# Latent attention and FFN on one core: when the main value products run among the score tiles

## The reference

```python
x = x + _layernorm(_L0_attn_ref(_layernorm(x), ...))
x = x + _layernorm(_L0_ffn_ref(_layernorm(x), ...))

# _L0_attn_ref, 16 heads of 128 + 64 (rope) query and key columns, 128 value columns:
scores = jnp.einsum('bhqd,bhkd->bhqk', qf, kf) * scale
probs = jax.nn.softmax(scores)
ctx = jnp.einsum('bhqk,bhkd->bhqd', probs, v)
main_out = ctx.transpose(0, 2, 1, 3).reshape(b, s, H * D_V) @ o_w.T
# beside it a second attention of 16 heads of 16 columns ("pattern"):
p_probs = jax.nn.softmax(jnp.einsum('bhqd,bhkd->bhqk', pq, pk) * PD ** (-0.5))
p_ctx = jnp.einsum('bhqk,bhkd->bhqd', p_probs, pv)
return gates[..., 0:1] * main_out + gates[..., 1:2] * pattern_out
```

## Time and profile before

| what | value |
|---|---|
| median of 3 runs | 790.09 us (786.98 to 792.28) |
| the profiled execution | 788.47 us, its span 786.7 us |
| PE busy | 751.6 us, 96% |
| DVE busy | 574.2 us, 73% |
| ACT busy | 391.9 us, 50% |
| POOL busy | 431.9 us, 55% |

### The profile page before, as it was taken

The page is one execution under the profiler, slowest core; times in us unless marked ns, Lnnn a source line. Parts: engine busy times, 40 slices in busy tenths (PEclk is TensorE's granted clock), DMA queues, the critical chain, the costliest instruction groups (busy, mean ns, idle before and its releaser), DMA issues. The chain is left out here.

```text
span 786.7 us, 13921 instructions
## 1 busy us (share of the span) xinstructions
PE 751.6 (96%) x5508; PEld 473.5 (60%) x5508; DVE 574.2 (73%) x674; ACT 391.9 (50%) x498; POOL 431.9 (55%) x281
## 2 busy tenths in 40 slices
PE   5998899999999999999999999999999999998995
PEld 5875565555555556655655565556655655457884
DVE  6886656775778577847774779577857789998647
ACT  4633455555555455555555555555555445641351
POOL 1253087437843794379437943794378445563343
PEclk9999999999999999999999999999999999998998
DMA  9897740044104430353045103530353312531001
GB/s 242 269 318 239 135 102 14 2 114 91 41 2 84 93 82 1 78 112 96 2 106 110 43 1 77 101 82 1 77 94 93 117 43 53 158 101 35 1 1 54
DMA packets 98169, 68.15 MB, mean 87 GB/s; under 512 B 66806, under 2 KB 76600, under 8 KB 97848
## 3 DMA queue, kind: packets, MB, share of 16 engines
q1 hardware_dynamic: 98104, 67.25, 34.2%
HBM read 41.23 MB, written 17.04 MB: 74 GB/s over the span
## 5 line engine op out<-in xcount | busy, mean ns | idle before, releaser
L1029 POOL TENSOR_TENSOR acc<-acc,em 128x1024 f32<-128x1024 f32 x96 | 234.8, 2446 | 55.0 <-ACT em L1086 52.6
L1170 DVE TENSOR_REDUCE m2p<-xb 128x2 f32<-128x1024 f32 x128 | 155.6, 1221 | 65.1 <-PE xb L1335 65.1
L1178 DVE TENSOR_REDUCE m<-xb 128x2 f32<-128x1024 f32 x128 | 155.8, 1221 | 61.9 <-PE xb L1335 61.5
L1077 ACT ACTIVATE ep<-xb 128x1024 f32<-128x1024 f32 x128 | 131.3, 1026 | 118.6 <-PE xb L1335 118.5
L1086 ACT ACTIVATE em<-xb 128x1024 f32<-128x1024 f32 x128 | 131.3, 1025 | 93.2 <-PE xb L1335 88.8
L1371 PE MATMUL pvm<-em,cpair 128*32 128x512 f32 x1024 | 136.0, 603 | 0.0
L992 POOL TENSOR_TENSOR rot<-rot,sin 128x512 f32<-128x512 f32 x32 | 41.1, 1285 | 121.1 <-DMA rot<-raw 121.1
L1335 PEld LDWEIGHTS xb<-pq,pk 49*128 49x128 f32 x256 | 23.8, 183 | 106.4 <-issue 88.8
L1029 POOL TENSOR_TENSOR acc<-em 128x1024 f32<-128x1024 f32 x16 | 38.2, 2390 | 84.1 <-PE xb L1484 75.9
L1382 PE MATMUL pvp<-ep,vp 128*32 128x512 f32 x512 | 66.6, 592 | 0.0
L1335 PE MATMUL xb<-pq,pk 49*128 49x512 f32 x256 | 64.1, 497 | 0.0
(11 more groups left out here) (283 smaller groups left out, 1304.9 us busy)
## 6 DMA issues: line engine op xcount, KB each, us to landing
rot<-raw SPq DMA_DIRECT2D x128, 64.0 KB, 2.3
pk<-spqk_d SPq DMA_DIRECT2D x48, 128.0 KB, 4.2
sums<-rec_d SPq DMA_DIRECT2D x32, 128.0 KB, 2.9
ctx_d<-ctxr SPq DMA_DIRECT2D x14, 256.0 KB, 2.0
pq<-spqk_d SPq DMA_DIRECT2D x48, 64.0 KB, 2.3
wraw<-wst_d SPq DMA_DIRECT2D x7, 384.0 KB, 5.5
em<-in_o_w SPq DMA_DIRECT2D x1, 2048.0 KB, 7.9
vp<-vp_d SPq DMA_DIRECT2D x8, 256.0 KB, 4.7
```

The lines of the kernel that those rows point to most:

```text
L1029: pool.tensor_tensor(acc[:, :, :], before, em[:, j:j + 2, :], ALU.add).then_inc(added, 1)
L1077: act.activation(ep[:, j:j + 2, :], src[:, :, :], ACT.Exp, scale=PAT_SCALE).then_inc(ep_ready, 1)
L1170: dve.tensor_reduce(m2p[:, 2 * tp:2 * tp + 2, t, kt], src[:, :, :], AX, ALU.max).then_inc(x_dve, 1)
L1178: dve.tensor_reduce(m2[:, q, :, t, kt], src[:, :, :], AX, ALU.max).then_inc(x_dve, 1)
```

## The change

In rounds 1 to 8 the main values that stood at the end of half steps 2, 4, 6, 10, 12 and 14 are not run there. They run at the end of the next half step, right ahead of that one's own main values. No instruction is added or removed, and no other engine's program changes; 6 x 8 = 48 groups of values move on PE.

```diff
+def together(v, s):
+
+    return s in (2, 4, 6, 10, 12, 14)
+
@@
                     if s == 0 and v >= 2:
                         main_values(v - 2, NS - 1)
-                    if s and 1 <= v <= NP:
+                    if s and 1 <= v <= NP and not together(v, s):
+                        if together(v, s - 1):
+                            main_values(v - 1, s - 2)
                         main_values(v - 1, s - 1)
```

## The result

The changed kernel takes 809.76 us (median of 4 runs, 808.66 to 811.42) against 790.77 (4 runs of the kernel before, 786.98 to 792.28): a ratio of 1.026, 95% interval 1.022 to 1.029. It is slower by 19 to 20 us (19.0 by the medians); the forecast was 808 us. The profiled execution took 808.66 us, its span 806.9.

The account below looks back on a forecast made before the run. The prediction took PE's sequence, and its waits for x buffers, to bound the attention part. Its terms summed as 788.47 - 0.7 (round 8) + 20.7 (rounds 1 to 7) = 808.5 us, stated as 808; range 799 to 815, chance 0.70.

Parts of the forecast that it names:

- What bounds the kernel: Attention rounds 1 to 7: PE, busy in 540 of 548 us, sets the time through its sequence and its buffer waits.
- The price of a group: A moved group of values on PE frees 1.17 us, adds 0.89, gains 0.28 on paper; 48 moves give 13.4 us.
- Rival 2: It cancels out: a second main group in a row costs 0.6 us, not 0.89, giving 796 to 790 us; chance 0.13.
- What the freed time meets: Odd half steps, rounds 1 to 7: tiles held by x buffer releases, so the six moves cost 3.45 us per round.
- Half steps 2 and 3: M3 already waits for DVE's reduction of mm11 and can't start earlier, so this move costs a net +0.89 us.
- What comes back: Half steps 4 to 7: M4's 0.54 and mm15's 0.52 us waits vanish, DVE's reductions ungroup; +2.78 us per round in all.
- the ledger: The prediction's sum of gains and costs for each moved group, place by place: 20.7 us over rounds 1 to 7.
- Round 8: Buffers free 1.8 us or more ahead in most half steps; five of six moves give 0.28 us; counted as -0.7.
- Rival 1: Fewer changes pay: third tile's buffer free 0.89 us or more ahead, each move gives 0.28, 775 us; chance 0.09.
- Rival 3: DVE falls behind: its reductions ungroup in half steps 4 and 12 too, giving 816 us and up, to 825; chance 0.08.
- Two signs in the list: Expected profile: PE waits ahead of T13, M3, M5, M7, M11, M13, M15, some 15 to 25 us; PE's busy time falls.
- The 6.6 us of waits: PE's waits in rounds 1 to 7 before the change, 2.5 + 2.2 + 1.9 us, expected to become 15 to 25.

## Why the prediction was right

**What bounds the kernel** held: PE's sequence, and next to it the release of the buffers. It lacked the third thing, the turned transfer. The forecast's difference, +20.0, meets +19.2 in the traces from round 1's start on, and 19.0 or 20.2 in the times; the extra 1.0 us ahead of round 1 was no part of it.

**The price of a group** held. Two main groups take 1.74 us (486.91 to 488.65), 0.87 each, where 0.89 was taken from main ahead of pattern values. Rival 2 rested on 0.6, a price that no row had, and falls. The Trainium skill's rule in "TensorEngine Tiling (Array Packing)", Key Properties, is that a change of tiling mode drains the engine. The runs agree where the buffers are free and a change is saved: 0.26 to 0.27 us a move in half steps 12 to 15 with shortened emptying, 0.3 in round 8 with full.

**What the freed time meets** held to a tenth of a microsecond a place. Two terms were mis-sized. First, each new wait costs PE about 0.1 us more than its length, because the first pair behind a wait takes 0.33 us and not 0.24 (M13's, 484.63 to 484.96). I had left that out: half steps 10 to 15 cost 0.31, 0.56 and 0.37 us a round in place of 0.26, 0.50 and 0.28. Second, in half step 10 the group frees 0.86 us and not 1.17, as it stands behind S0; this didn't show, since the buffers behind it allowed 0.63 at most.

**Half steps 2 and 3**, +0.89 a round: on average 0.84 came, but from 0.3 to 1.5, by the landing of the transfer; that the average came so near is partly luck. The term was right in size; its reason, that M3 alone holds, was half of it.

**What comes back** held: M4's and mm15's waits are gone, DVE's reductions are ungrouped, and half steps 4 to 7 cost 7.3 us where the ledger has 7.1.

**Round 8**: -0.7 was forecast, and with round 8 alone changed the trace has -0.7 up to the epilogue. Its make-up was another, though: four moves gained 0.3, one nothing, and the one in half step 2 cost 0.6, which the forecast had not seen. The changed kernel has -1.4 up to the same point, since M1's wait for DVE (0.4 us) in half step 1 is gone too. The times don't resolve either.

**Rival 1** named its point of decision, a buffer free 0.89 us ahead. With the buffers emptied sooner the loss is gone and half steps 12 to 15 gain, and in round 8, where the buffers are free, four of six moves gain as they stand. So the rival's mechanism is sound, and its condition is what rounds 1 to 7 don't meet. **Rival 3** saw a real mechanism only where the forecast had it, in half step 6. Two signs in the list were wrong. T3, pm3 and T7 wait as well, while M5, M11 and M13 have none in the list: they start within 0.07 us of their release, as the tile ahead of each has waited already. And PE's busy time did not fall but grew by 4.8 us. The groups' own rows fell from 136.0 to 126.2 us, but pairs behind a wait last 0.5 to 0.62 us in place of 0.40, which counts as busy. The 6.6 us of waits that the prediction starts from lack the 1.0 for `ep`; no term used it.

## What to carry to other kernels

Work that stands between two stretches of tiles may be the cover for the emptying of their buffers; before moving it, read for each tile behind it when its buffer is released, and compare that slack with the time to be freed. Merging two groups saves one change of kind but adds the whole group where nothing needs cover, so it pays only where the slack behind the first place is more than the length of the added group (0.87 us here). A transfer that waits in a queue behind loads that nobody needs yet can be the bound of a few half steps even where PE is 96% busy: reordering one issue gained more than any order of the values.

## What the runs showed of the hardware

- A wait of PE inside a stream of matmuls costs about 0.1 us beyond its length: the first pair behind it takes 0.33 us in place of 0.24, and 0.47 where it is the first pair of an mm tile (441.27 to 441.74 in round 5 of the kernel before).
- With the moved groups left out, the granted clock fell from 2.4 to 1.2 GHz for 3.4 us in mid attention, once, behind waits of PE of 0.42, 0.38 and 0.51 us, and the round became 1.6 us longer. With the transfer issued by ACT it fell twice, behind waits of 1.9 and 1.8 us, and not in the five rounds with waits of 1.3 to 1.6. The changed kernel, with 51 waits of up to 0.5 us in its rounds, kept the full clock in all of them; what tells these cases apart stays open.
- The same transfer, issued 7.9 to 9.6 us after a round's start, landed between 13.5 and 16.0 us in different rounds of one execution (2 to 7 of the kernel before). Issued by ACT from 5.5 us on, it still landed at 13.8 to 14.5, and the four issues hold ACT's own work for 2.4 us.
